# Placing rows for 32 experts in fixed stretches of 6400 rows, and scattering them at the end of the second graph layer

## What is computed

```
xn = _layernorm(x)
x = x + gnn(edge_index, edge_type, xn) + mix(xn)          # two graph layers, one attention
xf = _layernorm(x)
idx = argmax(xf @ router_w.T + router_b)                  # one of 32 experts for each node
h = relu(xf @ W1[idx] + b1[idx])                          # 256 -> 64
x = x + relu(h @ W2[idx] + b2[idx])                       # 64 -> 256
```

## Time and profile before

| what | us |
|---|---|
| time, median of 3 runs (lowest, highest) | 3642.26 (3624.54, 3656.19) |
| the profiled execution: its time | 3671.97 |
| its span | 3670.3 |
| last gather of the second layer issued | 3358.2 |
| last product of a sum of the second layer | 3405.0 |
| last rank written by DVE | 3421.6 |
| first scatter into `bucket` | 3430.1 |
| last scatter into `bucket` issued | 3494.8 |
| first product on a tile of the experts | 3517.3 |
| last scatter of the output issued | 3662.4 |

### The profile page before, as it was taken

One profiled execution on the slowest core, in us unless ns is written; L12 is line 12 of the kernel. 1 busy time (PEld: TensorE's weight loads), 2 busy tenths in 40 slices (PEclk: granted clock), 3 DMA queues, 4 the chain that ended last, 5 costly groups with the idle time before them and its releaser, 6 DMA issues. The chain is left out here.

```text
span 3670.3 us, 37811 instructions
## 1 busy us (share of the span) xinstructions
PE 2411.8 (66%) x9589; PEld 1740.0 (47%) x9592; DVE 918.3 (25%) x2885; ACT 658.9 (18%) x1463; POOL 1644.3 (45%) x1712
## 2 busy tenths in 40 slices
PE   7999346666676666666578356666566666667288
PEld 3677234544454444444456245445445454445145
DVE  2210112222212121122123023333233233234333
ACT  4455101111111111101111101111111111110033
POOL 0000645444544444454442555555555555553444
PEclk9999678877887788788789677777777777788697
DMA  7664523333333333333332323323323323222333
GB/s 219 227 225 185 157 89 113 106 104 100 115 105 98 99 110 106 105 102 109 99 113 82 114 80 87 90 83 88 88 85 88 87 85 90 84 84 62 110 106 94
DMA packets 155520, 401.34 MB, mean 109 GB/s; under 512 B 35102, under 2 KB 86657, under 8 KB 140348
## 3 DMA queue, kind: packets, MB, share of 16 engines
q0 software_dynamic: 81648, 219.65, 20.6%
q10 hardware_dynamic: 36156, 126.22, 9.0%
q1 hardware_dynamic: 37585, 53.92, 5.4%
HBM read 262.69 MB, written 141.04 MB: 110 GB/s over the span
## 5 line engine op out<-in xcount | busy, mean ns | idle before, releaser
L486 POOL DMA_INDIRECT gnn_ring<-table,g_idx x1564 | 1508.7, 965 | 1693.2 <-PE gnn_pagg L529 925.4
L529 PE MATMUL gnn_pagg<-gnn_ring,gnn_oh 128*128 x3904 | 1120.3, 433 | 354.4 <-issue 304.4
L529 PEld LDWEIGHTS gnn_pagg<-gnn_ring,gnn_oh 128*128 128x128 f32 x3904 | 780.9, 213 | 695.0 <-issue 578.2
L513 DVE TENSOR_TENSOR gnn_oh<-gnn_col,g_dst 128x256 f32<-128x256 f32 x976 | 410.2, 426 | 1754.3 <-DVEq L48 1511.4
L714 PE MATMUL gnn_pm<-gnn_whigh,gnn_high 128*128 128x512 f32 x392 | 202.9, 518 | 496.1 <-ACT gnn_rows L768 494.4
L768 ACT COPY gnn_rows<-gnn_pm 128x512 f32<-128x512 f32 x196 | 111.1, 587 | 1330.2 <-DMA pre_bs<-in_L_gnn_bases 1086.7
L714 PEld LDWEIGHTS gnn_pm<-gnn_whigh,gnn_high 128*128 128x128 f32 x392 | 95.2, 243 | 534.3 <-ACT gnn_rows L768 513.3
L1025 ACT ACTIVATE gnn_qe<-gnn_pq,gnn_bq 128x128 f32<-128x128 f32 x98 | 36.0, 367 | 1089.7 <-remote 1042.4
L714 PE MATMUL gnn_pm<-gnn_wlow,gnn_high 128*128 128x512 f32 x392 | 189.5, 483 | 0.0
L714 PE MATMUL gnn_pm<-gnn_whigh,gnn_low 128*128 128x512 f32 x392 | 189.1, 482 | 0.0
L365 PE MATMUL pre_psum<-pre_whigh,pre_high 128*128 128x512 f32 x392 | 158.6, 404 | 10.8 <-DVE pre_low L293 6.3
(11 more groups left out here) (172 smaller groups left out, 2306.5 us busy)
## 6 DMA issues: line engine op xcount, KB each, us to landing
table<-pre_rows ACTq DMA_DIRECT2D x49, 1024.0 KB, 3.9
table<-gnn_rows ACTq DMA_DIRECT2D x48, 1024.0 KB
gnn_ring<-table,g_idx POOLq DMA_INDIRECT x1564
pre_bs<-in_L_gnn_bases SPq DMA_DIRECT2D x64, 240.0 KB
bucket<-gnn_zrow SPq DMA_DIRECT2D x16, 650.0 KB
g_xT<-bucket SPq DMA_DIRECT2D x20, 520.0 KB
x1T<-gnn_x1T ACTq DMA_DIRECT2D x49, 128.0 KB
gnn_x1T<-x1T ACTq DMA_DIRECT2D x49, 128.0 KB, 2.2
```

Source lines behind the costliest of these rows:

```text
L486: eng.indirect_dma_start(self.ring[:, q % RG, t, 0:D], None, self.g.table[self.l][:, :], bass.IndirectOffsetOnAxis(ap=self.g.idx[:, at:at ...
L513: self.nc.vector.tensor_tensor(self.oh[:, h, :, :], self.col[:, :].unsqueeze(1).to_broadcast([P, n, P]), self.g.dst[:, ds(q * TPG + h * n, ...
L529: mm = nc.tensor.matmul(pagg[:, k, 0:self.width], self.oh[:, h, i, :], self.ring[:, ds(q & (RG - 1), 1), t, 0:self.width].rearrange("p o n ...
```

## The change

The places in `bucket` no longer depend on counts. Each expert has its own 6400 rows (CAP), enough for all 6250 nodes, and the table grows to 32 x 6400 + 128 rows.

- A product more in each rank of `gnn_second` (`ecap`) adds CAP times the expert's number to the rank, which is thereby the place. DVE casts it to an integer in the same step (`r.posi`) and raises `placed`.
- POOL issues the 49 scatters behind its last gather, in the block of `gnn_second`. It waits once for 38 ranks and then issues 38 scatters without a wait; each of the last 11 waits for its own rank.
- `gnn_second` and `experts` are one block. Instead of the clearing and the barrier each engine waits for `left`.
- Only the first 128 rows of each expert (and the 128 spare ones) are filled beforehand: 8 DMAs of 4 x 128 rows and one of 128, for 16 of 5 x 128.
- An expert's last tile takes the expert's last 128 rows, so that it overlaps the tile before it; DVE works out a mask `skip` and, in each tile, one more operation on 128 x 1 puts doubled rows out of range.
- The first row of each tile is data (`rowi`), so SP reads it into registers and issues one DMA to a tile, 80 for 20. It waits for `tiles_ok` before the first.
- DVE's work before the tiles loses the places and gains operations on 128 x 2560 elements: one comparison, two products and three sums for one comparison and one sum on 1 x 2560.

```
+CAP = 6400
-        self.bucket = dram("bucket", (MAXT * P, ROW), F32)
+        self.bucket = dram("bucket", (E * CAP + P, ROW), F32)
@@ gnn_first, sync
-                if q % 12 == 6 and q // 12 < XS:
-                    eng.dma_start(g.bucket[c * ZT * P:(c + 1) * ZT * P, :].rearrange("(t p) d -> p t d", p=P), ...)
+                c, at = divmod(q, 20)
+                if at == 6 and c < FILLS:
+                    first = g.bucket[0:E * CAP, :].rearrange("(e c) d -> c e d", c=CAP)[0:P, c * EF:(c + 1) * EF, :]
+                    eng.dma_start(first, zrow[:, :].unsqueeze(1).to_broadcast([P, EF, ROW])).then_inc(zeroed, 16)
+                elif at == 6 and c == FILLS:
+                    eng.dma_start(g.bucket[E * CAP:, :], zrow[:, :]).then_inc(zeroed, 16)
@@ gnn_second
+        SURE = NB - 12
         def _(eng):          # gpsimd
             agg.gather(eng)
+            for b in range(NB):
+                if b == 0 or b > SURE:
+                    eng.wait_ge(g.placed, max(b, SURE) + 1)
+                eng.indirect_dma_start(g.bucket[:, :], bass.IndirectOffsetOnAxis(ap=r.posi[:, b:b + 1], axis=0),
+                                       r.x2[:, b, :], None).then_inc(g.scattered, 16)
+                if b == NB - 5:
+                    eng.sem_inc(g.nearly, 1)
+                if ranked:   # vector
+                    V.tensor_copy(r.posi[:, ds(n - 6, 1)], r.rank[:, ds(n - 6, 1)]).then_inc(g.placed, 1)
             agg.end(eng)
+            eng.wait_ge(g.placed, NB)
+            eng.sem_inc(g.left, 1)
                 if there(-5):  # tensor
-                    nc.tensor.matmul(po[:, k, D:D + E], g.one[:, :], r.acc[:, j, :], start=True, stop=False)
+                    nc.tensor.matmul(po[:, k, D:D + E], g.one[0:2, :], ecap[:, :], start=True, stop=False)
+                    nc.tensor.matmul(po[:, k, D:D + E], g.one[:, :], r.acc[:, j, :], start=False, stop=False)
@@ experts, sync
-            eng.wait_ge(scattered, 16 * NB)
-            for c in range(MAXT // XG):
-                eng.dma_start(xb[:, lo:lo + XG, :], g.bucket[c * XG * P:(c + 1) * XG * P, :]...)
+            eng.wait_ge(tiles_ok, 1)
+            eng.wait_ge(scattered, 16 * NB)
+            for t in range(MAXT):
+                if t % XG == 0:
+                    at = values(rowi[0:1, t:t + XG], engines=[eng.engine], min_val=0, max_val=E * CAP, ...)[1]
+                if t >= XS:
+                    eng.wait_ge(landed[t % XS], 16 * (t // XS))
+                eng.dma_start(xb[:, t % XS, :], g.bucket[ds(at[t % XG], P), :]).then_inc(x_in[t % XS], 16)
@@ experts, gpsimd
-            for b in range(NB):
-                if b == 0 or b == EARLY:
-                    eng.wait_ge(pos_ok, 1 if b == 0 else 2)
-                eng.indirect_dma_start(g.bucket[:, :], ... posi[:, b:b + 1] ..., r.x2[:, b, :], None).then_inc(scattered, 16)
@@ experts, tensor (unchanged but for the name of nearly)
             eng.wait_ge(tiles_ok, 1)
             eng.wait_ge(w_in, 32)
-            eng.wait_ge(nearly, 1)
+            eng.wait_ge(g.nearly, 1)
             for n in range(WARM):
@@ experts, vector
+                node = x[:, D:D + 1].bitcast(I32)
+                V.tensor_tensor(node, node, skip[:, t:t + 1], ALU.max)
@@ program
-        nc.clear_and_free_semaphores(nc.allocated_since(had))
-        nc.all_engine_barrier()
```

112 lines of the change are left out of this document (63 added, 49 removed).

## The result

The changed kernel takes 3682.66 us (median of 4 runs, 3678.53 to 3690.04), the kernel before beside it 3633.4 (4 runs, 3608.93 to 3656.19): a ratio of 1.0129, 95% interval 1.0076 to 1.0182. It is slower by 49 us, and its interval lies above 1; forecast was 3641, with a range of 3596 to 3664 and no change, and slower had 0.08. The profiled execution took 3684.35 us, its span is 3682.6.

What follows compares the result with a forecast made beforehand. POOL and PE together pace the second layer; then counts, scatters, loads and WARM run serially before the tiles. First tile product at 3515.2 for 3517.3, plus 2 us in the loop, sums to 0: 3641 us, range 3596 to 3664.

Steps and rivals of the forecast that it cites:

- Scatters: POOL behind its last gather: 40 unbroken scatters into bucket, 1.27 us each, 50.8 us from 3359.1.
- The hold: Second layer's tail: POOL's unbroken indirect DMAs starve PE, so the last rank comes at 3464 instead of 3421.8.
- the 8 us that were to be done early: Second layer's tail: 8 of PE's 58.6 us of work done early, 50.6 remaining after POOL's run.
- Barrier, preparation, WARM: Between last rank and first tile: barrier gains 1.2 us, DVE's preparation takes 23.6 us, WARM 27.6 us.
- Loads: Expert stage: 80 loads for 20, each 0.36 us of issue plus unpriced register work, cost nothing.
- Expert stage unchanged, 153 us: Tiles at 1.58 us each; DVE's added operation fits its idle time, so 153 us as before.
- a clock of 0.50 from early in the stage: Expert stage: granted clock low from early on, named as a sign that the prediction is wrong.
- Additions in the loop: Second layer's loop: one small PE product and one DVE cast in 49 steps, 0 to 10 us, taken as 2.
- Rival 3: Expert stage slower: single loads or longer DVE turn drop the clock early, 1.05 us more a tile, up to 3715; chance 0.07.

Runs made afterwards that it cites:

- e13: Changed kernel with its 80 loads made 20 again, each of 4 tiles at places known beforehand; 3667.65 us, ratio 1.0045 to the kernel before.
- e1: Changed kernel with one more unread product (bf16, 128x512) behind the two transposes of each tile; 3623.68 us, ratio 0.9954.
- e10: Kernel before with the same wide unread product in each tile as e1; 3656.88 us, ratio 0.9914.
- e14: Changed kernel with DVE's added operation on doubled rows made once for four tiles; 3680.1 us, ratio 1.013.
- e3: Changed kernel with POOL's 80 output scatters replaced by plain DMAs on SP's queue, rows not going to their nodes; 3598.64 us, ratio 0.9858.
- e15: Changed kernel with one DVE operation of 128x768 added in each tile; 3623.25 us, ratio 0.9962.
- after: First profile of the changed kernel as it stands; the profiled execution took 3684.35 us.
- e2: Changed kernel with its first 41 scatters into bucket in bursts of 8, each behind one more rank; 3638.67 us, ratio 0.9899.
- e7: Changed kernel with the wide unread product only in tiles 24 to 79; 3759.98 us, no ratio given.
- e8: Changed kernel with 37 scatters into bucket among the second layer's gathers, the last 12 behind the last gather; 3736.81 us, ratio 1.0145.
- e9: Changed kernel with two DVE copies (128x256 and 128x128) added in each tile; 3725.35 us, ratio 1.0114.
- e12: Changed kernel with all 49 scatters into bucket behind the last rank; 3712.85 us, ratio 1.0073.
- e5: Changed kernel, unchanged, for more runs and a second profile; 3730.1 us, ratio 1.0142.
- e18: The version of e11 once more, where the kernel before takes 2621.56 us; 2615.57 us, ratio 0.9979.
- e11: Changed kernel with scatters in bursts of 8, a wide unread product in each tile, and WARM 24 for 116; 3628.65 us, ratio 0.9852.
- e17: Changed kernel with 20 four-tile loads at known places and the doubled-rows operation once per four tiles; 2598.34 us, ratio 0.9911.

## Why the prediction was wrong

The steps, with what the changed kernel's profile showed:

1. *Scatters:* right. 40 unbroken ones in 50.8 us, from 3307.3.
2. *The hold:* the mechanism right, the size too small by 9 to 12 us. Gather to counts grew from 65.1 and 68.3 to 119.4, 51 to 54 us; 42 had been put down. PE did 6.69 us of work in 50.8 us (forecast: 6 in 47), but it resumed 7.2 us behind POOL's last scatter, not 3, and the 8 us that were to be done early saved nothing: from its resumption to the counts it took 60.2 us, as long as the whole had taken in the first profile of before (3363.2 to 3423.3).
3. to 5. *Barrier, preparation, WARM:* right. From the count product to the first tile 50.6 us; forecast 51.2 from DVE's start. Preparation 3425.6 to 3449.2, 23.6 us as summed; WARM 26.8 us for 27.6.
6. *Loads:* waits for them come to 2.9 us in all. Right as a cost; by e13 they may bear on how early the clock falls.
7. *Expert stage unchanged, 153 us:* **the step that failed.** From the first product on a tile to the end of the span the changed kernel took 206.5 us. The step was put at 1.58 us a tile from one profile in which the clock fell 110 us into the stage (and 1.58 was itself a mean of tiles of 1.43 us and of pauses). That was read as the stage's way of working; it was luck. In the second profile of before the clock fell at 41 us and the same stretch took 193.6 us. In the changed kernel it fell at 22 us, and 64 tiles ran at 2.63 us. The prediction named a clock of 0.50 from early in the stage as a sign of being wrong, and gave it 0.07.
8. *Additions in the loop:* whatever they cost is hidden by the difference between executions.

Put together by the columns of the table: gather to first tile is 170.0 against 159.1 and 162.8, 7 to 11 us lost, where the sum had 2 gained. That leaves some 40 of the 49 us for the earlier fall. This is a remainder, but two runs bear it out: with the clock held by the same product the changed kernel has a ratio of 0.9954 (e1) and the kernel before 0.9914 (e10), 0.4% or 15 us apart in place of 1.3% (each of the two intervals reaches 0.3 to 0.4% to either side). Rival 3 was the one that came, by its place (the clock in the expert stage) and price (1.05 us a tile), but not by DVE's longer turn (e14 took it back, and the ratio stayed at 1.013); its other cause, the single loads, is not excluded (e13). What takes the clock down is one pause of PE, DVE and ACT together, which goes away with POOL's output scatters (e3) or with a longer tile (e1, e15). This is taken to be the hold of step 2, seen in the layer and not looked for in the stage, where the profile had five pauses of PE of 0.9 to 1.1 us (3558.62, 3567.11, 3575.39, 3617.54, 3626.02), the last of them just ahead of the fall at 3627.8:

```profile
3626.02 0.44 PE L1137 MATMUL exp_psum<-g_ident,exp_xf 128*128 128x128 f32 x2 [1.11 <-DVE g_xT L1195]
...
3627.76 0.63 PE L1137 MATMUL exp_psum<-g_ident,exp_xf 128*128 128x128 f32 x2
```

The prediction had no rival from that row.

What stays open: why in the changed kernel six of seven profiles of its stage have the fall 22 to 26 us behind the first tile (after, e2, e7, e8, e9, e12; e5 at 48.7), while before it came at 41 and 110. e13 (3 of 10 runs 37 to 50 us under its median) suggests the single loads; how the stage is entered was not separated from them. And where the hold comes from is shown only from outside: it lies beside POOL's unbroken indirect DMAs, it halves when they come in bursts (e2), goes when none lies beside the layer's last sums (e12), each costs its own time or more among the gathers (e8), and it is absent in e18, whose kernel is e11's.

The Trainium skill (Runtime: NRT & Kernel Launch, Instruction fetch mechanics) has sequencers fetch their instructions by DMA, mostly hidden. In the changed kernel PE, DVE and ACT had next to no work for 48 us while POOL issued, and PE's gap is put down to its sequencer ("PEq"); a fetch that is not hidden could look like this, and where e17 and e18 have the same work, PE shows no such gap. No run measured the fetch itself, so this stays a guess.

## What to carry to other kernels

Before work is moved beside another engine's, find in the trace what the mover does to bystanders when it runs without a pause; here, outside the last set, each scatter beside the layer cost it 1.27 us or a little more (unbroken, or among the gathers; in bursts half of that, e2), so an early start gained nothing and e12's late one was faster. A time that depends on the clock in one profile is one draw: take a second profile of the kernel before, and compare the spread of its runs with the price of the fall. Where one engine needs nearly as long for a tile (here POOL, 1.28 us) as the tile takes (1.43), a few tenths of a microsecond more to a tile can pay: in e1 they took 61 us off a stage of 194.

## What the runs showed of the hardware

- The clock went from 1.00 to 0.50 behind a pause of PE of 0.7 to 2.2 us, in a loop where PE was busy 93% of the time, and did not return in 165 us of PE busy 100% (after), nor in 144 us of 98% with a wide product a tile (e7). Twenty-four unread 128x512 products took it up in e11. In e18 it returned 4.8 us into the tiles, at their start.
- The same pause often leaves it up: 1.50, 1.49, 1.57 passed, 1.55 did not (e14). The Trainium skill (TensorE: Matmul & The Clock Gate, HAM oscillation) has a loop in which PE's waits for DMA, 3 to 5 us each, throttle it every time. The pauses here are shorter, and which of them took the clock down looks like chance.
- Over the first four sets the kernel before took 3604 to 3730 us (but for the one execution at 11576), and in the last set 2621 us, with the granted clock at 0.78 to 0.81 and at 0.93. How much PE works beside POOL's DMAs differs between these levels, by the two pairs of windows above; the rest of the difference was not taken apart.
